# Attention by groups of four heads, with the next group's scores interleaved, in a two-layer recurrent kernel

## The reference

```python
xn = layernorm(x)                                   # layer 0
s = scan(h = tanh(h @ A + u @ Bm)) ... @ W_out      # 512 steps, state of 64
g = silu(tanh(x @ wo.T + c_final @ uo.T + bo))      # c_final from a second scan of 64 steps
x = x + s * g
xn = layernorm(x)                                   # layer 1
q, k, v = xn @ W.T * 256**-0.5, in 16 heads of 16   # causal softmax(q k / 4) v
s = heads @ W_proj.T / 16
g = silu(mixture of the 2 nearest of 32 low-rank experts(xn))
return x + s * g
```

## Time and profile before

| | us |
|---|---|
| median of 3 runs | 1225.31 (1222.66 to 1225.59) |
| the profiled execution: its own time | 1227.31 |
| its span, first to last instruction | 1225.5 |
| PE / DVE / ACT / POOL busy | 1069.8 / 510.6 / 488.5 / 256.6 |
| mean granted PE clock | 0.936 of 2.4 GHz |

### The profile page before, as it was taken

One profiled execution on the slowest core, in us unless ns is written; L12 is line 12 of the kernel. 1 busy time (PEld: TensorE's weight loads), 2 busy tenths in 40 slices (PEclk: granted clock), 3 DMA queues, 4 the chain that ended last, 5 costly groups with the idle time before them and its releaser, 6 DMA issues.

```text
span 1225.5 us, 20586 instructions
## 1 busy us (share of the span) xinstructions
PE 1069.8 (87%) x6848; PEld 708.9 (58%) x6848; DVE 510.6 (42%) x1028; ACT 488.5 (40%) x1198; POOL 256.6 (21%) x237
## 2 busy tenths in 40 slices
PE   4699999999997557898799799889889889979986
PEld 2267777777775334555555565555555545546644
DVE  4611211212122233644744743653663564565461
ACT  2334444444444202263263264255246336326234
POOL 2200101101004223222321420521322322422000
PEclk8899999999998768899899999989989989989989
DMA  6530101011030075058039019119308506705700
GB/s 212 174 102 29 51 26 51 29 48 49 28 111 18 34 107 99 19 100 159 18 77 181 18 59 153 46 52 129 94 35 128 112 18 112 145 18 93 96 19 18
DMA packets 80501, 93.99 MB, mean 77 GB/s; under 512 B 9920, under 2 KB 72032, under 8 KB 80480
## 3 DMA queue, kind: packets, MB, share of 16 engines
q1 hardware_dynamic: 76256, 89.52, 35.1%
q10 hardware_dynamic: 4224, 4.19, 1.0%
HBM read 59.84 MB, written 33.59 MB: 76 GB/s over the span
## 4 chain that ended last, share of the span: by engine, by line
PE 70%; DVE 10%; issue 7%; ACT 5%; DMA 4%; SPq 2%; POOL 1%; DVEq 0%; ACTq 0%; POOLq 0%
PE PS L708 22%; PE PS L844 5%; PE PS L781 5%; PE PS L922 5%; PE PS L887 5%; DVE nm L1451 5%; PE PS L865 3%; PE PS L695 3%; PE PS L811 3%; PE PS L759 3%; DMA XT<-xt_d 2%; PE PS L948 2%; PE PS L790 2%; PE PS L889 2%; ACT arena L1184 2%
## 5 line engine op out<-in xcount | busy, mean ns | idle before, releaser
L708 PE MATMUL PS<-arena 128*128 128x256 f32 x1024 | 312.1, 421 | 0.0
L1451 DVE TENSOR_REDUCE nm<-PS 128x2 f32<-128x256 f32 (+3 forms) x256 | 200.9, 817 | 90.3 <-PE PS L867 89.3
L695 PEld LDWEIGHTS PS<-arena 128*72 128x72 f32 x1024 | 129.9, 141 | 68.1 <-ACT arena L1069 4.6
L1069 ACT ACTIVATE arena<-PS 64x8 f32<-64x8 f32 x512 | 88.5, 173 | 185.1 <-PE PS L695 181.4
L708 PEld LDWEIGHTS PS<-arena 128*128 128x128 f32 x1024 | 155.5, 192 | 0.0
L865 PE MATMUL PS<-K,Q 96*128 96x128 bf16 (+3 forms) x512 | 129.8, 319 | 25.0 <-DVE nm L1451 20.5
L1184 ACT ACTIVATE arena<-PS 128x1024 f32<-128x1024 f32 x128 | 128.5, 1029 | 29.2 <-PE PS L889 28.6
L887 PE MATMUL PS<-Q,K 98*128 98x512 bf16 (+3 forms) x512 | 122.8, 318 | 16.6 <-DVE nm L1451 14.1
L1311 DVE SCALAR_TENSOR_TENSOR arena<-arena 128x512 f32<-128x512 f32 x16 | 11.1, 694 | 267.7 <-ACT arena L1080 267.7
L695 PE MATMUL PS<-arena 128*72 128x8 f32 x1024 | 121.3, 191 | 0.0
L867 PE MATMUL PS<-negmask,identb 128*128 128x128 bf16 x512 | 105.6, 228 | 0.0
(11 more groups left out here) (161 smaller groups left out, 1399.9 us busy)
## 6 DMA issues: line engine op xcount, KB each, us to landing
qk_d<-QB SPq DMA_DIRECT2D x24, 512.0 KB, 2.9
Q<-qk_d SPq DMA_DIRECT2D x96, 128.0 KB, 8.9
K<-qk_d SPq DMA_DIRECT2D x96, 128.0 KB, 9.5
X<-in_L_attn_x SPq DMA_DIRECT2D x12, 512.0 KB, 13.5
arena<-xt_d SPq DMA_DIRECT2D x16, 256.0 KB, 3.2
gt_d<-arena SPq DMA_DIRECT2D x16, 256.0 KB, 2.5
wx_d<-arena SPq DMA_DIRECT2D x16, 256.0 KB, 2.0
XT<-xt_d SPq DMA_DIRECT2D x8, 512.0 KB, 9.9
```

What stands on the lines that cost most here:

```text
L695: pe.matmul(PS[0:WIDE, 7, 0:B], w_ab, HB[:, step], start=True, stop=True).then_inc(c_mm.sem, 1)
L708: mm = pe.matmul(o, lhs, rhs, start=first, stop=last)
L1451: v_.tensor_reduce(nm[:, i, 2 * hp:2 * hp + 2], PS[:, 2 * (u % 3):2 * (u % 3) + 2, 0:(i + 1) * P], AX.X, ALU.max, negate=True).then_inc(m_ ...
```

## The change

The batch is now four stages, one for each group of four heads. In stage g, PE makes the turned scores of group g in ten units of one bank (`turned`, k = 0 to 9), two in flight in banks 3 and 4, and between them the scores of the next group, two units after each of k = 0 to 4 and the eleventh after k = 5, in banks 0 to 2. At k = 7 `maxima_turn` turns the next group's maxima in one transpose, ACT and DVE cut them, and ACT's own queue sends them; the next stage's first unit waits for them to land. Stage 3 makes the scores of group 0 of the next batch. The values of a group are multiplied at k = 1 of the next stage. The steps of the following batches are dealt out over the stages: `leave`, `value`, `heads_turn`, `project` in stage 0; `normal_turn`, `query_key`, `distance` in stage 1; `experts` in stage 2; `mix` (two batches ahead) and `low_rank` in stage 3. The loads of XT, GT, WX and X1 run two batches ahead.

The feature order of q and k in DRAM becomes (dimension, head, token), so that four heads of a row are one run of 4 KB. A group's operands are six transfers (24 for a batch, as before), each with 16 outer rows. `value` writes `VA` on DVE directly (POOL's copy is gone), the mixture weights are turned in one transpose and taken by four copies, and the query and key weights are reordered once by two DVE copies.

```diff
+BLOCKS = [(0, 3), (3, 2), (5, 1)]
+ROWS = [(3, 0, 1), (3, 1, 1), (3, 2, 1), (3, 3, 1), (2, 0, 1), (2, 1, 1), (2, 2, 1), (2, 3, 1), (1, 0, 2), (1, 2, 2),
+        (0, 0, 4)]
+SU = len(ROWS)
+TQ = 5 * GH // 2
...
+                for at, n in BLOCKS:
+                    first = PAIRS[at][0]
+                    rows_of = slice(at * HD, (at + n) * HD)
+                    for dst, c, parts in ((Q6, 0, qk_d[first:first + 1, 0].broadcast_to([n, HD, H, T])),
+                                          (K6, 1, qk_d[0:n, 1])):
+                        sp.dma_start(dst[rows_of, heads, :], parts[:, :, heads].rearrange("r d h t -> d r h t")
+                                     ).then_inc(q_ld[g].sem, 16)
...
+            def scores(b, g, u):
+                i, h, n = ROWS[u]
+                bank = u % 3
+                if u == 0:
+                    pe.wait_ge(q_ld[g].sem, q_ld[g].at(b, 2 * len(BLOCKS)))
+                elif u == 2:
+                    pe.wait_ge(m_h.sem, m_h.at(b, g))
+                elif u > 2:
+                    pe.wait_ge(m_r.sem, m_r.at(b, g * SU + u - 2))
...
+            def turned(b, g, k):
+                if k == 0:
+                    pe.wait_ge(m_ld[g].sem, m_ld[g].at(b, 2))
+                pe.wait_ge(t_e.sem, t_e.at(b, g * TQ + k - 1))
...
+            def stage(b, g, side, nxt):
+                for k in range(TQ):
+                    turned(b, g, k)
+                    if nxt is not None:
+                        for u in (2 * k, 2 * k + 1):
+                            if u < SU:
+                                scores(*nxt, u)
+                        if k == 7:
+                            maxima_turn(*nxt)
+                    run(side, k)
...
+            def take_maxima(b, g):
+                heads = slice(g * GH, (g + 1) * GH)
+                act.wait_ge(m_a.sem, m_a.at(b, g + 1))
+                act.wait_ge(m_h.sem, m_h.at(b, g + 1))
+                for row, part_of in ((KS, nmh), (KS + 1, nml)):
+                    act.dma_start(Q6[row:row + 1, heads, :].rearrange("o h (i q) -> o (h i) q", q=P), part_of[:, g]
+                                  ).then_inc(m_ld[g].sem, 16)
...
+            def stage2(b, more, more2):
+                side = {2: [lambda: take_values(b, 1)], 7: [lambda: maxima_high(b, 3)],
+                        5: [lambda: expert_gate(b, 0)], 9: [lambda: expert_gate(b, 1)]}
+                if more2:
+                    side[0] = [lambda: hidden(b + 2, 0)]
+                    side[1] = [lambda: hidden(b + 2, 1)]
+                    side[3] = [lambda: hidden(b + 2, 2)]
+                    side[6] = [lambda: normal_again(b + 2)]
+                    side[7].append(lambda: open_gate(b + 2))
+                side[8] = [lambda: take_maxima(b, 3)]
...
+            def stage1(b, more, first=False):
+                side = {6: [lambda: divide(b, 0)]}
+                if not first:
+                    side[1] = [lambda: add_rows(b - 1)]
+                stage(side, (b, 2))
                 if more:
                     split(b + 1, 0, Q)
                     remainder(b + 1, 0)
...
                     split(b + 1, 2, Q)
...
                     distance(b + 1)
```

More of the change, by code:

```diff
@@ new lines, in stage3 @@
+            def stage3(b, more, more2):
+                side = {1: [lambda: values(b, 2)], 3: [lambda: values_turn(b, 2)]}
+                if more2:
+                    side.setdefault(1, []).append(lambda: mix(b + 2, 0, True))
+                    side.setdefault(2, []).append(lambda: mix(b + 2, 1, True))
+                if more:
+                    for j in range(NT):
+                        side.setdefault(3 + j, []).append(lambda j=j: low_rank(b + 1, j, more2))
+                        side.setdefault(4 + j, []).append(lambda j=j: low_rank_turn(b + 1, j, more2))
+                    side[8] = [lambda: weights_turn(b + 1)]
+                    for j in range(1, NT):
+                        side[3 + j].reverse()
+                stage(b, 3, side, (b + 1, 0) if more else None)
@@ L1237, in _, with stage, stage0 @@
-            act.wait_ge(init, 7)
+            def stage(b, g, side):
+                for k in range(TQ):
+                    exp(b, g, k)
+                    run(side, k)
+            def stage0(b, more, first=False):
+                side = {7: [lambda: maxima_high(b, 1)]}
+                if not first:
+                    side[2] = [lambda: take_values(b - 1, 3)]
+                    side[6] = [lambda: take_heads(b - 1)]
+                if more:
+                    side[9] = [lambda: normalise(b + 1)]
+                side[8] = [lambda: take_maxima(b, 1)]
+                stage(b, 0, side)
@@ new lines, in stage1 @@
+            def stage1(b, more, first=False):
+                side = {2: [lambda: take_values(b, 0)], 7: [lambda: maxima_high(b, 2)]}
+                if more:
+                    side[1] = [lambda: take_normal(b + 1)]
+                    for n in range(4):
+                        side.setdefault(3 + n, []).append(lambda n=n: take_query_key(b + 1, n))
+                    side[9] = [lambda: square(b + 1)]
+                side[8] = [lambda: take_maxima(b, 2)]
+                if not first:
+                    side.setdefault(4, []).append(lambda: store(b - 1))
+                stage(b, 1, side)
@@ L1238, in _, with stage3 @@
+            def stage3(b, more):
+                side = {2: [lambda: take_values(b, 2)]}
+                if more:
+                    for j in range(NT):
+                        side[4 + j] = [lambda j=j: take_low_rank(b + 1, j)]
+                    side[7].insert(0, lambda: maxima_high(b + 1, 0))
+                    side[8] = [lambda: take_maxima(b + 1, 0)]
+                    side[9] = [lambda: take_weights(b + 1)]
+                stage(b, 3, side)
+            act.wait_ge(init, 8)
             open_gate(0)
@@ L1239, in _ @@
             normal_again(0)
-            hidden(0)
+            for n in range(3):
+                hidden(0, n)
             normalise(0)
```

810 lines of the change are left out of this document (451 added, 359 removed).

## The result

Four executions of the kernel after took 1256.56 us in the median (1252.47 to 1257.42), four of the kernel before 1224.13 (1222.66 to 1225.59); the ratio is 1.0233, 95% interval 1.0197 to 1.0270. The interval lies wholly above 1, so the change makes the kernel slower, by 2.3%. The profiled execution has a span of 1255.3 us, 29.8 more than before, at a mean PE clock of 0.913.

What follows compares the result with a forecast made beforehand. PE bounds the kernel, 97.2 us a batch. PE work 81.5, idle 16.5 and slow clock 6.9 make 104.9 a batch; with the loop's ends and small waits, 1268 us. Range 1190 to 1310, the forecast's own 1235 to 1300.

Steps and rivals of the forecast that it cites:

- Stage 0 to 1: Handover of the maxima from stage 0 to stage 1: PE waits 0.5 us a batch.
- Stage 1 to 2: Handover of the maxima from stage 1 to stage 2: PE waits 2.1 us a batch.
- Stage 3 to 0: Handover from stage 3 to the next batch's stage 0: PE waits 3.2 us, maxima landing at t0 + 4.8 (t0: end of `maxima_turn`).
- DVE's queue behind stage 1: Next batch's splits and distances, 10.9 us on DVE, delay score unit 3 of stage 2: 5.4 us new PE wait.
- Stage 2 to 3: Handover from stage 2 to stage 3, maxima queued behind ACT's `normal_again` and `open_gate`: PE waits 3.5 us.
- Inside stage 3: `low_rank(1)` waits 1.4 us for `weigh(0)` on DVE, the next ones 0.1 to 0.2 each: 1.8 us together.
- The clock: PE's clock falls behind three waits a batch (after stages 1, 2 and 3), 2.3 us each: 6.9 us against 4.7.
- The work on PE: PE's own work a batch at 2.4 GHz: 81.5 us, 0.8 less through fewer transposes.
- Beside the path: Added work off PE's path: some 10 us more on ACT and 2 on DVE a batch, covered as a total.
- Rival 4: By the skill's rule on queues, sending the maxima by ACT does nothing; contained in the forecast, no time of its own.
- Rival 1: Interleaving wins, PE's side work covers the handovers: 93 us a batch, 1178 us in all; chance 0.25.
- Rival 3: Slow clock feeds itself, transfers landing at 4.1 us under operand loads: 115 us a batch, 1335 us; chance 0.13.

Runs made afterwards that it cites:

- the spread: Changed kernel with DVE's splits, remainders and distances behind stage 1 dealt out, partly ahead of `maxima_low`, partly between stage 2's reductions: 1241.45 us, ratio 1.0103.
- Quiet, with spread: Changed kernel with DVE's block behind stage 1 dealt out and SP holding back a save and loads until the maxima landed: 1192.49 us, ratio 0.9710.
- the filler: Changed kernel with 10 matmuls on constants a batch in PE's waits, to keep its clock up: 1223.26 us; with 20 of them 1259.31 us.
- three edits: Changed kernel with DVE's block dealt out, the maxima's chain one unit earlier, and bulk transfers held back until maxima landed: 1166.80 us, ratio 0.9498.
- SP sends: Changed kernel with the maxima sent from SP's queue in place of ACT's: 1247.39 us, ratio 1.0156.
- spread, early: Changed kernel with DVE's block behind stage 1 dealt out and the maxima's turn, copy, remainder and sends one unit earlier: 1188.25 us, ratio 0.9675.

## Why the prediction came out, step by step

**The sign and the mechanism were right; the size was right partly by two errors that cancel.** Forecast 1268, measured 1256.6. The five periods were 100.4 us instead of 104.9, 22.5 less in sum; the loop began at 470.9 instead of 466, and the two ends together took 7.5 more than I had summed.

- **Stage 0 to 1**: 0.5 forecast, no wait of 0.5 or more measured. My own terms give 4.6 - 4.4 = 0.2 there and not 0.5.
- **Stage 1 to 2**: 2.1, measured 1.25. **Stage 3 to 0**: 3.2, measured 2.05. The landing, 2.0 assumed and 1.7 in the median, is the smaller part of the error. In the period shown, the first send goes out 1.26 us after the turn in stage 1, where I had 1.9, and 1.65 after it in stage 3, where I had 2.1, and there PE's remaining work takes 2.0 us and not 1.5.
- **DVE's queue behind stage 1**: 5.4, measured 3.7 to 5.4, 4.5 in the mean; it is 5.4 where the clock stays up ahead of it and less where PE comes there late. The block is 10.0 us long, with a remainder of 3.03 beside POOL, as forecast, and the spread showed that the wait hangs on this block. The spread alone gets only half of it back: the splits done sooner brought saves and loads into the handovers, which the prediction looked for as lateness ("late next") and not as traffic.
- **Stage 2 to 3**: 3.5, measured 3.4, for the wrong reason. Two errors cancel. The first send goes out 3.6 us after `turned(6)` and not 5.3, since `open_gate`, charged at 1.15, doesn't hold it up; and the landing, charged at 2.0, took 4.2. Quiet, with spread, brings it to 1.3. The upper bound that I gave for the landing, 4.1, is about what this one stage shows.
- **Inside stage 3**: 1.8, measured 2.2.
- **The clock**: 6.9 us a batch forecast. Counted in the same way, 100.4 x (1 - 0.922) = 7.8 us are spent on it; the filler gives 5.0 of them back, and PE's busy time falls from 86.5 to 80.8 where no handover waits. I had three places in every batch. There are four in two of the five periods and two or three in the others: the clock always falls at the handover to stage 3 and at unit 3, and only sometimes behind the handovers to stages 2 and 0, at the same lengths of wait. So the sum is about right, and the reading under it, that the length of a gap decides, is not right.
- **The work on PE**: 81.5; 80.8 measured at a clock of 1.00. **Beside the path**: 10 us more on ACT and 2 on DVE forecast; busy time grew by 1.6 and 2.6, and ACT's eight issues take 4.5. It was covered, as forecast.
- **Rival 4, the sending by ACT does nothing**: failed. The Trainium skill (DMA: Bandwidth & Descriptors, "Issuing engines are not separate DMA queues") says that issuing from another engine saves only the sequencer's time. The runs agree in that it shortens no landing: the median is 1.7 us from either queue. The cost comes with ACT's own lateness, 0.43 us at the handover to stage 0; all together it is 0.8%.
- **Rival 1** (1178) needed idle and clock under 15.7 us a batch. By the 80.8 us of PE work the changed kernel has 100.4 - 80.8 = 19.6; with three edits to the order it has 88.1 - 80.8 = 7.3 and takes 1167 us. So the interleaving isn't slower as such: its handovers were laid out without slack. **Rival 3**'s long landing was real in one stage of four.

Taken one at a time: the layout gave the kernel before 0.8%. Undone alone in the changed kernel, the sends by ACT are worth 0.8%, the block on DVE 1.3%, and the late turn 3.1% (1.0233 against 0.9912). These don't add, since each takes waits that the others would leave, and the clock goes with all of them.

## What to carry to other kernels

When a stage can't begin until something small has landed, count the chain from its last input to landing, and place its start so early that PE's remaining work covers it: one unit of ten was worth 3% here. Hold bulk transfers back until the small one has landed. And count on a PE wait costing more than its length: 13.4 us of waits a batch came here with some 5 us of slow clock on top. But don't count on the clock falling at a given place, for behind equal waits it fell in one period and not in another.

## What was unexpected on the chip

- A transfer of 4 KB from 16 rows lands 1.7 us after its issue in the median and up to 4.3 beside SP's loads, although it is on another queue. The Trainium skill (DMA: Bandwidth & Descriptors, "Queues, rings and completion order") says that each DMA engine takes turns between queues by packets. The trace agrees in that traffic of one queue delays a transfer of another; the packets themselves it doesn't show. Holding a save back took 1.4 us out of one wait, holding loads back 2.8 out of another.
- ACT's queue issues a transfer while an activation ahead of it still runs (941.23 against 940.74 to 941.88).
- DVE operations on 128x4 elements took 2.15 and 2.17 us beside a POOL operation against 0.17 without. The Trainium skill (SBUF — State Buffer, "Who interferes with whom") has DVE operations of two SBUF inputs contend with a GpSimd operation that reads SBUF, and DVE's two-port modes fully blocked while a GpSimd operation that was issued first runs. The trace agrees: both of these began after POOL's and ended with it. The reciprocal, 0.18, was not delayed, though all but 0.02 us of it lay beside the second POOL operation.
- Whether a wait lowers the clock isn't a matter of its length alone. In the changed kernel the clock fell behind 1.25 us of waiting in one period and not behind 1.22 in the next; in "SP sends" it fell behind 1.15 to 1.19 in all five. At the handover to stage 3 in the run "spread, early" it fell behind 2.31 us once, and here PE had waited 2.50 us and it stayed at 1.00:

```profile
898.00:900.00 2.00, 0.00 (x0) 0.00 (x0) 0.69 (x1) 0.86 (x2) 0.00 (x0) 1.00 1.07 193
900.00:902.00 2.00, 1.76 (x14) 0.97 (x14) 1.00 (x2) 0.98 (x2) 0.00 (x0) 1.00 0.98 160
902.00:904.00 2.00, 2.00 (x26) 0.80 (x28) 1.49 (x3) 0.22 (x1) 0.00 (x0) 1.00 1.00 184
```

  What decides between them stays open.
